# Metaformer block (deformable attention, then a mixture of experts): gate scores taken from the token transposes, channels split from PSUM, batches written out

## What is computed

```python
v = _ln_c(x)                                   # normalise over the 96 channels
value, query = _dwconv(v, w_v, b_v, 1), _dwconv(v, w_q, b_q, 1)     # 3x3 depthwise
key, off     = _dwconv(v, w_k, b_k, 2), _dwconv(v, w_off1, b_off1, 2)
o = gelu(layernorm_over_channels(off) * ln_g + ln_b)
pos = tanh(einsum('bhwc,pc->bhwp', o, w_off2) + ref)
v_sampled = grid_sample_bilinear(value, pos)   # 784 samples per image
attn = einsum('bcm,bcn->bmn', query, key) * SCALE
x = x + einsum('bchw,oc->bohw', einsum('bmn,bcn->bcm', attn, v_sampled), w_out)
t = tokens(x)                                  # 3136 tokens of 96 channels
n = _ln_t(t)                                   # (t - mean) / sqrt(var + 1e-5)
probs = softmax(n @ gate_w + gate_b)           # 4 experts, the best two kept
h = gelu(n @ w1[e] + b1[e]);  y[e] = h @ w2[e] + b2[e]    # 96 -> 384 -> 96
x = from_tokens(t + sum_e gate[e] * y[e])
```

## Time and profile before

| | |
|---|---|
| median of 3 runs | 898.64 us (895.98 to 900.95) |
| span of the profiled execution | 894.8 us |
| TensorE busy | 775.4 us, 87% (matmul records), weight loads 57% |
| VectorE, ScalarE, GpSimd busy | 75%, 44%, 36% |
| chain that ended last | TensorE 51%, VectorE 23%, GpSimd 11%, issue 7%, ScalarE 3%, DMA 3% |
| mean granted TensorE clock | 0.929 of 2.4 GHz |

### The profile page before, as it was taken

The page is one execution under the profiler, slowest core; times in us unless marked ns, Lnnn a source line. Parts: engine busy times, 40 slices in busy tenths (PEclk is TensorE's granted clock), DMA queues, the critical chain, the costliest instruction groups (busy, mean ns, idle before and its releaser), DMA issues.

```text
span 894.8 us, 10704 instructions
## 1 busy us (share of the span) xinstructions
PE 775.4 (87%) x3304; PEld 514.3 (57%) x3304; DVE 670.5 (75%) x1397; ACT 396.8 (44%) x726; POOL 322.5 (36%) x184
## 2 busy tenths in 40 slices
PE   2899779759997898988997798989996998999996
PEld 1454445645664456655664455755663556588885
DVE  6789769899896487878896587899882354667775
ACT  2322412424555107542555106544542134599995
POOL 2000700007777001127677002148897011234443
PEclk9998979559998899998999799999997996999998
DMA  9103401201232001261132001151422000221111
GB/s 179 44 0 108 108 1 54 55 34 39 91 103 79 7 4 36 82 160 39 60 127 83 8 0 39 47 133 42 148 72 78 0 25 16 87 70 55 62 55 31
DMA packets 17312, 55.12 MB, mean 62 GB/s; under 512 B 5008, under 2 KB 8720, under 8 KB 15216
## 3 DMA queue, kind: packets, MB, share of 16 engines
q1 hardware_dynamic: 12656, 39.90, 15.8%
q10 hardware_dynamic: 1536, 9.84, 3.3%
q0 software_dynamic: 3072, 4.82, 2.1%
HBM read 35.07 MB, written 14.65 MB: 56 GB/s over the span
## 4 chain that ended last, share of the span: by engine, by line
PE 51%; DVE 23%; POOL 11%; issue 7%; ACT 3%; DMA 3%; DVEq 0%; ACTq 0%; SPq 0%; POOLq 0%
PE py L615 10%; POOL big L1215 8%; PE pd L555 7%; DVE query L919 6%; PE pa L430 4%; PE ph L470 4%; PE pd L535 3%; POOL x L1225 3%; PE pd L578 3%; PE ph L630 3%; PE ph L631 2%; PE ph L632 2%; DVE key_area L919 2%; DVE big L919 2%; PE ph L653 2%
## 5 line engine op out<-in xcount | busy, mean ns | idle before, releaser
L1225 POOL TENSOR_TENSOR x<-x,ye 96x448 f32<-96x448 f32 x112 | 240.1, 2144 | 464.8 <-DVE ye L1143 461.3
L830 ACT ACTIVATE hid<-ph,b 128x448 f32<-128x448 f32 x252 | 159.0, 633 | 263.8 <-PE ph L632 261.0
L615 PE MATMUL py<-hid,w 128*96 128x448 f32 x504 | 241.0, 560 | 31.5 <-DVE ye L1143 24.4
L630 PE MATMUL ph<-x_hi,w_hi 96*128 (+1 forms) x252 | 169.7, 673 | 0.0
L1143 DVE SCALAR_TENSOR_TENSOR ye<-py,b,gate_all 96x448 f32<-96x448 f32 x112 | 75.3, 677 | 53.0 <-PE py L615 25.3
L615 PEld LDWEIGHTS py<-hid,w 128*96 128x96 f32 x504 | 82.1, 168 | 55.8 <-DVE ye L1143 16.6
L1215 POOL DMA_INDIRECT big<-value_table,rows x64 | 77.3, 1208 | 88.4 <-DMA value_table<-xT 69.2
L631 PE MATMUL ph<-x_lo,w_hi 96*128 (+1 forms) x252 | 94.8, 376 | 0.0
L632 PE MATMUL ph<-x_hi,w_lo 96*128 (+1 forms) x252 | 94.3, 374 | 0.0
L919 DVE SCALAR_TENSOR_TENSOR big<-xpad,conv_w,big 96x3136 f32<-96x3136 f32 (+1 forms) x28 | 90.0, 3215 | 4.7 <-issue 4.3
L919 DVE SCALAR_TENSOR_TENSOR query<-xpad,conv_w,query 96x3136 f32<-96x3136 f32 (+1 forms) x28 | 93.1, 3324 | 0.5
(11 more groups left out here) (136 smaller groups left out, 1089.8 us busy)
## 6 DMA issues: line engine op xcount, KB each, us to landing
gate_all<-gate_rows SPq DMA_DIRECT2D x56, 336.0 KB, 3.1
value_table<-xT ACTq DMA_DIRECT2D x8, 1176.0 KB, 7.2
xs<-in_x SPq DMA_DIRECT2D x4, 1176.0 KB, 8.5
x<-in_x SPq DMA_DIRECT2D x4, 1176.0 KB, 7.9
x<-x SPq DMA_DIRECT2D x4, 1176.0 KB, 6.9
out<-x SPq DMA_DIRECT2D x28, 168.0 KB, 2.0
big<-value_table,rows POOLq DMA_INDIRECT x64
big<-in_w SPq DMA_DIRECT2D x1, 576.0 KB
```

The lines of the kernel that those rows point to most:

```text
L615: nc.tensor.matmul(py[e % 2][0:C, 0:GPIX], w2[:, c, :], hid[:, k % 3, :], start=(j == 0), stop=(j == CPE - 1)).then_inc(hid_used, 1)
L630: nc.tensor.matmul(bank, w1_hi[:, cols], xh[:, px], start=True, stop=False)
L830: nc.scalar.activation(hid[:, k % 3, :], ph[k % 2][:, 0:GPIX], ACT.Gelu, bias=b1[:, k % NCH:k % NCH + 1]).then_inc(hid_act, 1)
L1225: ins = p.tensor_tensor(r, r, ye[:, e, :], ALU.add)
```

## The change

- **Scores from the transposes.** A new constant `ident_gate` (96 x 100) holds the identity and, in four more columns, `gate_w` less its mean over the channels. "x1T" multiplies each token tile by it in a plain matmul, so each token gets its 96 channels and four raw scores. The tokens go to a tile `x1T` that lies in `big`. VectorE scales the raw scores by `rstd` and adds the bias right behind the normalising (four operations before `normalise_off`). The 28 score matmuls are gone, and the scores' use of a `pd` bank.
- **Split from PSUM.** "x1c" goes to `pd` banks. ScalarE rounds a group from PSUM straight into `x_hi`, and VectorE forms `x_lo` from PSUM less `x_hi` in one operation, which frees the bank. `xc` and VectorE's copy are gone.
- **The tables.** In `ROUND` all seven groups of "x1c" stand before chunk 66 (spread 0; it was 66 with spread 4), "score" is gone, "exp" moves from 74 to 70, "gateT" from 79 to 77. In `LAST_ROUND` "x1c" stands before 67 with spread 0 (it was 2), "exp" moves from 77 to 70, "gateT" from 82 to 78. `normalise_off` gets no outputs among it.
- **Batches written out.** Rounds 1 and 2 are no hardware loop any more, and all counts are constants.
- **In the head**, a small matmul forms the mean of `gate_w`, and VectorE waits for it before it splits w1.

```diff
-         ("offT", 58, 0, 27), ("x1T", 60, 2, 0.5), ("keyT", 62, 0, 1), ("x1c", 66, 4, 12), ("score", 71, 0, 13),
-         ("exp", 74, 0, 4), ("gateT", 79, 0, 9), ("offc", 79, 0, 0), ("offs", 82, 0, 0), ("tanh", 83, 0, 5),
+         ("offT", 58, 0, 27), ("x1T", 60, 2, 0.5), ("keyT", 62, 0, 1), ("x1c", 66, 0, 12), ("exp", 70, 0, 0), ("gateT", 77, 0, 12), ("offc", 79, 0, 0), ("offs", 82, 0, 0), ("tanh", 83, 0, 5),
-              ("x1c", 67, 2, 10), ("score", 72, 3, 10), ("exp", 77, 0, 4), ("gateT", 82, 0, 6), ("end", 84, 0, 1)]
+              ("x1c", 67, 0, 10), ("exp", 70, 0, 0), ("gateT", 78, 0, 12), ("end", 84, 0, 1)]
...
-        xc = big[0:C, :]
+        x1T = big[0:TP, 0:NT * XC].rearrange("p (t c) -> p t c", c=XC)
...
+                nc.tensor.matmul(py[0][0:C, 0:EXPERTS], mean_of, gate_w[:, :], start=True, stop=True).then_inc(gate_mean, 1)
...
-                    transposes(bank, [x[:, (GRP * g + k) * TP:(GRP * g + k + 1) * TP] for k in range(GRP)], C, TP).then_inc(act_full, 1)
+                    for k in range(GRP):
+                        last = nc.tensor.matmul(bank[0:TP, k * XC:(k + 1) * XC], x[:, (GRP * g + k) * TP:(GRP * g + k + 1) * TP], ident_gate[:, :], start=True, stop=True)
+                    last.then_inc(act_full, 1)
...
                 chunks_to(plan.at("x1c"))
-                score_bank = dve_bank(b, "score")
...
-                channels_back(b, "x1c", x1_normed, x1_normed_act, before_x1c)
...
+                for g in range(NG):
                     chunks_to(plan.at("x1c", g))
+                    if g < NORM_DVE:
+                        pe.wait_ge(x1_normed, b * NORM_DVE + g + 1)
+                    else:
+                        pe.wait_ge(x1_normed_act, b * (NG - NORM_DVE) + g - NORM_DVE + 1)
+                    bank = dve_bank(b, "x1c", g)
+                    transposes(bank, [x1T[:, GRP * g + k, 0:C] for k in range(GRP)], TP, C).then_inc(dve_full, 1)
...
-            with pe.Fori(0, BATCH - 2) as b:
+            for b in range(BATCH - 2):
...
                 def channels(g):
                     gelus_to(plan.at("x1c", g))
-                    empty(b, "x1c", g, xc[:, g * GPIX:(g + 1) * GPIX], C, GPIX)
-                normalise(b, x1_stats, x1_normed_act, channels)
+                    i, full = dve_job(b, "x1c", g)
+                    act.wait_ge(dve_full, full)
+                    nc.scalar.activation(xh[:, half(b) + g * GPIX:half(b) + (g + 1) * GPIX], pd[i][0:C, 0:GPIX], ACT.Copy).then_inc(x_high, 1)
+                normalise(b, x1T, x1_stats, x1_normed_act, channels)
...
                 dve.wait_ge(consts_in, NCONST)
+                dve.wait_ge(gate_mean, 1)
+                v.tensor_tensor(ident_gate[:, C:XC], gate_w[:, :], py[0][0:C, 0:EXPERTS], ALU.subtract).then_inc(gate_centred, 1)
                 link(v.tensor_copy(w1_hi[:, :], w1))
...
+                link(v.tensor_tensor(sc[:, :, :], x1T[:, :, C:XC], full(rstd[0:TP, :]), ALU.mult))
+                link(v.tensor_tensor(sc[:, :, :], sc[:, :, :], gate_b[:, :].rearrange("p (o e) -> p o e", o=1).to_broadcast([TP, NT, EXPERTS]), ALU.add))
+                link(v.tensor_reduce(mx[:, :], sc[:, :, :], AX.X, ALU.max))
+                v.tensor_tensor(sc[:, :, :], sc[:, :, :], full(mx), ALU.subtract).then_inc(score_ready, 1)
                 if with_head:
 
                     dve.wait_ge(x1_normed_act, (b + 1) * (NG - NORM_DVE))
-                    normalise_off(b + 1, turn)
+                    normalise_off(b + 1, no_turn)
...
-                        dve.wait_ge(act_done, acted(b, "x1c", g))
...
-                        link(v.tensor_copy(xh[:, to], xc[:, px]))
-                        v.tensor_tensor(xl[:, to], xc[:, px], xh[:, to].bitcast(f32), ALU.subtract).then_inc(x_split, 1)
-                        turn(0.9)
+                        dve.wait_ge(x_high, b * NG + g + 1)
+                        to = slice(half(b) + g * GPIX, half(b) + (g + 1) * GPIX)
+                        v.tensor_tensor(xl[:, to], pd[dve_job(b, "x1c", g)[0]][0:C, 0:GPIX], xh[:, to].bitcast(f32), ALU.subtract).then_inc(dve_done, 1)
```

More of the change, by code:

```diff
@@ L39 @@
 HCH = 128
+XC = C + EXPERTS
 NCH = EXPERTS * HID // HCH
@@ L57 @@
 ACT_REST = (jobs("valT", NG) + jobs("xT", NG) + jobs("xc", NG) + jobs("mix", QUARTERS) + jobs("offT", 2)
[L58 removed]
+            + jobs("x1T", NG) + jobs("keyT", 2) + jobs("gateT", 1) + jobs("offc", 2))
 DVE_HEAD = jobs("offs", 1)
[L61 to L63 removed]
+DVE_REST = jobs("kv", QUARTERS) + jobs("y", NY) + jobs("x1c", NG) + jobs("offs", 1)
 CHUNKS = NG * NCH
@@ L291, in job @@
             last = [j for j in rest if j not in head]
-            static = isinstance(b, int)
             if (name, g) not in head:
-                order = last if static and b == BATCH - 1 else rest
+                order = last if b == BATCH - 1 else rest
                 i = order.index((name, g)) + len(head)
-            elif static and b == 0:
+            elif b == 0:
                 i = head.index((name, g))
@@ L299, in job @@
                 i, b = rest.index((name, g)) + len(head), b - 1
-            return i % 2, b * len(rest) + i + 1
-        assert len(ACT_REST) % 2 == len(DVE_REST) % 2 == 0
+            i += b * len(rest)
+            return i % 2, i + 1
         def first(b):
-            return isinstance(b, int) and b == 0
+            return b == 0
         def act_job(b, name, g=0):
@@ L562, in rest @@
                 chunks_to(plan.at("x1T"))
+                if first(b):
+                    pe.wait_ge(gate_centred, 2)
                 for g in range(NG):
@@ L571, in rest @@
                 chunks_to(plan.at("x1c"))
-                score_bank = dve_bank(b, "score")
[L574 to L583, removed]
-                    chunks_to(plan.at("x1c", g))
-                channels_back(b, "x1c", x1_normed, x1_normed_act, before_x1c)
[L587 to L590, removed]
-                last.then_inc(dve_full, 1)
+                for g in range(NG):
+                    chunks_to(plan.at("x1c", g))
+                    if g < NORM_DVE:
[4 more added lines that the diff above has]
+                    transposes(bank, [x1T[:, GRP * g + k, 0:C] for k in range(GRP)], TP, C).then_inc(dve_full, 1)
                 chunks_to(plan.at("gateT"))
@@ L842, in _ @@
             rest(0, True, PLAN, lambda number: None)
-            with act.Fori(0, BATCH - 2) as b:
+            for b in range(BATCH - 2):
                 gelus_to = experts(b)
@@ L892, in statistics, with norm_tokens @@
                 turn(1.9)
-            def norm_tokens(b, name, back, eps, stats, normed, turn):
+            def norm_tokens(b, src, name, back, eps, stats, normed, turn):
                 for g in range(NG):
@@ L1070, in rest @@
                     turn(0.0, "keyT")
-                norm_tokens(b, "x1T", "x1c", LN2_EPS, x1_stats, x1_normed, turn)
+                norm_tokens(b, x1T, "x1T", "x1c", LN2_EPS, x1_stats, x1_normed, turn)
+                full = lambda m: m[:, :].rearrange("p (t o) -> p t o", o=1).to_broadcast([TP, NT, EXPERTS])
+                link(v.tensor_tensor(sc[:, :, :], x1T[:, :, C:XC], full(rstd[0:TP, :]), ALU.mult))
+                link(v.tensor_tensor(sc[:, :, :], sc[:, :, :], gate_b[:, :].rearrange("p (o e) -> p o e", o=1).to_broadcast([TP, NT, EXPERTS]), ALU.add))
@@ L1128, in rest @@
                 turn(0.0, "end")
-                assert not with_head or n[0] == (FIRST_REST_STEPS if first(b) else REST_STEPS), n[0]
             def experts(b):
@@ L1193, in _ @@
             rest(0, True, no_turn)
-            with dve.Fori(0, BATCH - 2) as b:
+            for b in range(BATCH - 2):
                 outputs_to = experts(b)
```

55 lines of the change are left out of this document (24 added, 31 removed).

## The result

The changed kernel takes **911.72 us** (median of 4 runs, 908.4 to 912.18), the kernel before 897.31 us (median of 4, 895.96 to 900.95): 1.014 times as long, 95% interval 1.010 to 1.018. The forecast was 914 us, its range 898 to 924, with 0.72 on slower. The profiled execution of the changed kernel took 912.1 us, its span is 910.3 us; before, the span was 894.8 us. So 15.5 us have to be found in the spans. In every run that gives both, the time lies some 1.8 us above the span, as it does here.

A forecast was written before the change was run, and what follows sets the result against it. Rounds were taken as nearly full on TensorE, with VectorE and the gates following it at a round's end. Terms 20 - 5 - 1 + 1 = +15 us on the 894.8 us span, plus 3.8 to the median, gave 914 us; range 898 to 924.

The forecast's parts named there:

- The wait on the bank: Rounds 1 and 2, TensorE at group 2 of "x1c": 11.2 us idle until VectorE's first split behind `normalise_off`.
- +10 us a round: Rounds 1 and 2: TensorE's delay reaches VectorE through the offsets, +10 us each (7 to 13), +20 together.
- The signs named: Round lengths named as evidence beforehand: rounds 1, 2 and 3 some 10, 5 and 0 us longer.
- it now waits for the offsets: VectorE before `pz`: its own work is some 6 us later, so it waits for TensorE's offsets at about 603.5.
- Gain 5 us (4.3 to 6.6): Start of round 2: without the loop's jump VectorE's 4.33 us stand goes, and late outputs add 0 to 2.3 us.
- Gain 1 us: Round 3, no `normalise_off` there: only the bank turns hold TensorE, gain 1 us (-3 to +1.5).
- Batch 0: No chunks there: `normalise_off` ends at 173.0 as before, bank turns and the exponential follow; cost 1 us (0 to 1.5).
- The token product: "x1T" as plain matmuls: 0.71 us a group against 0.41, taken as 1.8 us more a round (1 to 3).
- rival (3): "x1T": plain matmuls cost four times the transposes, 6.8 us more each than taken, 934 us; chance 0.03.
- (1): Rival: the bank wait never bites, TensorE keeps its clock, each round gains 3 to 4 us, 888 us; chance 0.12.
- (2): Rival: waits before `kv` absorb most of TensorE's delay, rounds at +3 to +5, 900 to 904 us; chance 0.13.

The follow-up runs named there:

- Split ahead: The changed kernel with VectorE's seven splits moved ahead of `normalise_off` instead of behind it: 894.16 us, 0.995 of the kernel before.
- second trace of before: The kernel before, unchanged, profiled once more: 897.02 us, span 895.2 us.
- the loops alone: The kernel before with its three hardware loops written out and nothing else: 883.82 us, 0.982 of before.
- the scores alone: The kernel before with loops written out and token-product scores; transposes back still go through `pa` into `xc`, spread over four chunks: 881.78 us.
- the one piece: The kernel with the scores alone, its seven groups of "x1c" in one piece ahead of chunk 66 (67 in round 3): 890.59 us.
- the kernels with `pa` banks: Transposes back go through `pa` into SBUF: the scores alone, 881.78 us, and that kernel with ScalarE writing both `x_hi` and `xc`, 877.79 us.

## Why the prediction was right, step by step

The number was right, by 2 us, and so was the mechanism of the loss. That the number came so close is in part luck: of the terms, some held, and the loops and the rest were off in opposite directions.

The sum on the spans was +15.0, measured +15.5. I then put the median 3.8 us above the span and took that for what lies around it; what lies around it is some 1.8 us in every run, and the other 2 are that the profiled execution of before was one of its shorter ones.

**The wait on the bank held.** 11.2 us forecast, 11.32 and 11.32 measured in rounds 1 and 2; two of its terms were off and cancelled, the score operations with 2.1 us (357.81 to 359.90) for 1.25 and `normalise_off` with 6.6 (360.10 to 366.66) for 7.2. The last transposes were to end 6.8 us after the splits began, measured 6.4 (366.57 to 372.94, the row at 371.99); splits 1.0 to 1.3 us apart, measured 2.33 a pair; the clock at 0.50 behind it. "Split ahead" shows that the order behind it is the cause: turned round, it gives back 17.6 us.

**+10 us a round held in size, not in its path.** Measured 10.9 and 10.3 against the second trace of before, 8.4 and 7.2 against the first. From `pz` to `pz`, which the start of `kv` doesn't enter, round 1 is 9.9 to 10.2 us longer and round 2, with the loop's gain in it, 3.3; round 3 and all behind it is 0.8 shorter. The signs named were 10, 5 and 0. The step that failed is "it now waits for the offsets": VectorE came to `pz` 10 us late by itself, held by outputs of late chunks (8.9 us, the rows above). I had followed VectorE's own operations and the gates, and left out that outputs stand among them, of which each waits for a chunk. The offsets themselves ended at 401.1, so without those outputs VectorE would have had to wait for them, until 0.7 us before the time at which it came. Both paths were late by nearly the same.

**"Gain 5 us (4.3 to 6.6)" for the loops was mis-sized.** The stand of 4.33 us is gone, and the stretch with the jump is 7.0 us shorter against the second trace (3.8 against the first); with the loops alone out, the spans differ by 9.6 to 10.0 and the medians by 15.6. I had taken nothing for the rest of the loop. VectorE's register instructions, some 240 a turn in the loop and none in the straight code, are a candidate for it, and the trace bears it out in part. In the stretch with the jump VectorE needs 101.3 us from `pz` to its first work on gathered rows in the second trace of before (388.94 to 490.26), and 94.3 with the loops out (388.16 to 482.48). Of these 7.0 us the stand is 4.44; beside it VectorE has thirteen idle times of 0.2 to 0.4 us there, 3.4 us together, all but one ended by no other engine, and the straight code has none of them. One of them, in which the trace has three register instructions, and the same output in the straight code:

```profile
406.36 0.68 DVE L1143 SCALAR_TENSOR_TENSOR ye<-py,b,gate_all 96x448 f32<-96x448 f32 x1 [0.36 <-DVE w L979]
```

```profile
401.61 0.68 DVE L1143 SCALAR_TENSOR_TENSOR ye<-py,b,gate_all 96x448 f32<-96x448 f32 x1
```

No run leaves the jump and takes out the register instructions, so how the whole 15.6 divide stays open.

The Trainium skill, "Runtime: NRT & Kernel Launch", section "Instruction fetch mechanics", says that a taken branch to a target outside the pages at hand has to fetch it before the engine goes on, and gives that as one reason to unroll. The trace agrees in so far as VectorE stands at the jump, 4.33 us in the earlier trace rows and 4.44 us in the second trace; at the end of round 2, where the loop is left, it goes on without a stand (the row is of the second trace). That it fetches at the jump no view of this case shows, and the page gives no figure for it.

```profile
598.89 4.05 DVE L919 SCALAR_TENSOR_TENSOR big<-xpad,conv_w,big 96x3136 f32<-96x3136 f32 x1
```

**"Gain 1 us" for round 3 held as a sum of two larger terms that I had too small.** With the scores alone the last stretch is 191.4 us, 6.7 less than before (198.05 in the first trace, 198.11 in the second); with the one piece and the bank turns it is 197.5 again. I had 5.8 - 1.8 for the scores and thus some 3 for the turns; the runs have some 6.7 and 6.1.

**Batch 0** cost 2.8 instead of 1, and by another path. I had `normalise_off` end at 173.0 as before; it ended at 175.8. VectorE already begins to normalise the tokens 2.6 us later behind `kv` (44.7 for 42.1): the token product starts 1.4 us later, and it takes 6.1 us where the transposes took 4.1 with their waits. Before, then after:

```profile
160.42 3.92 DVE L906 TENSOR_SCALAR xT<-xT,mean,rstd 112x96 f32<-112x96 f32 x16
```

```profile
163.22 3.92 DVE L902 TENSOR_SCALAR big<-big,mean,rstd 112x96 f32<-112x96 f32 x16
```

Group 2 does wait here too, 10.17 us, but from this point to the sums the change costs only some 0.2 us against before (20.9 us before, 21.1 after, 19.5 with the scores alone, so 1.6 against that one).

**The token product** was dearer than taken. Its rows in round 1 (three groups, three, one):

```profile
338.35 2.62 PE L573 MATMUL pa<-ident_gate,x 96*112 96x100 f32 x24
342.20 2.62 PE L573 MATMUL pa<-ident_gate,x 96*112 96x100 f32 x24
346.04 0.94 PE L573 MATMUL pa<-ident_gate,x 96*112 96x100 f32 x8
```

These are 6.2 us for seven groups against 3.2 before: +3.0, the upper bound, where I took 1.8. A group is 0.87 to 0.94 us, about twice the 0.41 of the transposes, and rival (3) falls with it. The Trainium skill, "TensorE: Matmul & The Clock Gate", section Terms, calls the transpose mode four times faster for FP32; by that, as an estimate, a group would have been 1.64 us, which these rows don't bear out.

**Where the two errors met.** By medians the change is -15.6 (loops), -2 (scores), +8.8 (one piece), +21.1 (banks): +12 against the 899 of the experiments. My sum had -5 for the loops and +20 for all else, where the medians have -15.6 and +27.9. So both were too small, by 11 and by 8 us, and that they cancelled is luck. In the spans all else is +25.1 against the loops alone (910.3, 885.2). Of these, 11.8 and 12.0 lie in the parts with "x1c" (102.52 and 102.65 against 90.70), where I had 10 each, 3.0 in batch 0, and -1.7 in the last stretch, where I had -1.

**The rivals.** (1), the wait that never bites, is what the kernels with `pa` banks show: 878 to 882 us, better than its 888, though a gain in the rounds through TensorE, which I gave it, isn't there. (2), the slack before `kv`, falls: what follows `pz` waits for the gather, and that starts from VectorE. Behind the late `pz` of round 2 the next `kv` takes 102.90 us after and 103.14 before; behind that of round 1 it takes 105.41, and 104.28 with the loops alone. So nothing of a late `pz` was made up there.

## What to carry to other kernels

A bank that engine A frees hangs on everything that stands ahead in A's queue; before such a hand-over is moved, list what stands there (here 6.6 us of `normalise_off`), and ask who runs behind the engine that waits. Two PSUM banks with two readers in a row behind each were dear in every order tried here (888 to 912 us against 882), least where other matmuls stood between the groups and VectorE was free; a copy into SBUF by a less busy engine, ScalarE at 45%, was cheaper, with no bank waiting for the busy one. And cost a hardware loop as a whole by writing it out alone: the visible stand at its jump was less than half of what it cost.

## What was not expected of the hardware

ScalarE stands of 2 to 6 us in the transposes back, while GpSimd issues the gather, ended mostly by what the profile calls another core or an unknown queue (`remote`; 4.42, 5.03, 5.14 us in the rows above). They are in the trace of the changed kernel and of every experiment, and in the second trace of before, but not in its first, and the time of before is the same, 897.0 us with a span of 895.2, with them. What they are stays open.

The loop's jump stopped more than the engine that stood: in the second trace of before VectorE's stand is followed by TensorE, which waits 4.94 us (4.80 in the first trace) for an output that VectorE owes it.

```profile
398.70 3.48 DVE L919 SCALAR_TENSOR_TENSOR big<-xpad,conv_w,big 96x3136 f32<-96x3136 f32 x1 [4.44 <-issue]
...
407.10 1.81 PE L615 MATMUL py<-hid,w 128*96 128x448 f32 x2 [4.94 <-DVE ye L1143]
```
